# Layer 0 of a two-layer kernel: two DRAM places for the query and key halves, doubled key rows, and a new place for the weight loads and for GpSimd's low halves

## What is computed

```python
def _L0_xattn_ref(X, encoder_output, causal_mask, padding_mask, Wq, bq, Wk, bk, Wv, bv, Wo, bo):
    q = X @ Wq.T + bq                     # 32 heads of 8, in 8 groups of 4
    k = encoder_output @ Wk.T + bk        # 8 groups of 8
    v = encoder_output @ Wv.T + bv
    ...
    scores = jnp.einsum('bgrqd,bgkd->bgrqk', q, k) / jnp.sqrt(jnp.float32(HD))
    scores = jnp.where(causal_mask[None, None, None, :, :], -jnp.inf, scores)
    scores = jnp.where(padding_mask[:, None, None, None, :], -jnp.inf, scores)
    w = jax.nn.softmax(scores, axis=-1)
    out = jnp.einsum('bgrqk,bgkd->bgrqd', w, v)
    ...
    return out @ Wo.T + bo

def hbitlinear(x, w, bits):               # layer 0's feed-forward part: up, relu squared, down
    xq = act_quant(fwht(x), bits)         # Hadamard transform, then 8-bit rounding by the row's maximum
    wq = weight_quant(w)
    return jnp.einsum('bsd,fd->bsf', xq, wq)

x = x + jnp.tanh(g_xattn[0]) * _L0_xattn_ref(_layernorm(x, axis=-1), ctx_2048, ...)
x = x + jnp.tanh(g_ffn[0]) * _L0_ffn_ref(_layernorm(x, axis=-1), L0_ffn_w_up, L0_ffn_w_down)
```

## Time and profile before

| | us |
|---|---|
| median of 3 runs | 1274.64 (1269.18 to 1277.73) |
| the profiled execution | 1274.92 |
| its span, first to last instruction | 1272.9 |
| busy: PE, DVE, ACT, POOL | 1126.0, 1059.2, 918.8, 736.3 |
| mean granted TensorE clock | 0.967 |

### The profile page before, as it was taken

How to read it: one execution, slowest core, us unless ns; L and a number is a source line. 1 busy time by engine, 2 the same in 40 slices (tenths; PEclk the granted TensorE clock), 3 DMA queues, 4 the chain that set the end, 5 groups by cost and what they waited for, 6 DMA issues and landing times. The chain is left out here.

```text
span 1272.9 us, 30350 instructions
## 1 busy us (share of the span) xinstructions
PE 1126.0 (88%) x8831; PEld 909.1 (71%) x8831; DVE 1059.2 (83%) x2469; ACT 918.8 (72%) x3601; POOL 736.3 (58%) x1084
## 2 busy tenths in 40 slices
PE   2688888877899999999999999999899999659992
PEld 2345555544588888888888888888787788549981
DVE  6689999988798898998898888899689888766664
ACT  3556666658899889989989989987788888213330
POOL 5357777776756665665665665665445787323331
PEclk9889999999999999999999999999899999879996
DMA  6445554442230312220330220220311100633326
GB/s 165 88 81 78 84 77 79 76 69 49 72 105 1 88 32 57 87 66 21 87 87 0 87 87 0 87 87 31 110 52 59 35 35 31 254 95 82 96 68 202
DMA packets 135320, 97.04 MB, mean 76 GB/s; under 512 B 59070, under 2 KB 128832, under 8 KB 135233
## 3 DMA queue, kind: packets, MB, share of 16 engines
q1 hardware_dynamic: 125680, 84.18, 26.6%
q0 software_dynamic: 3408, 8.45, 1.8%
q10 hardware_dynamic: 6144, 3.35, 0.9%
HBM read 55.02 MB, written 41.56 MB: 76 GB/s over the span
## 5 line engine op out<-in xcount | busy, mean ns | idle before, releaser
L1543 POOL TENSOR_TENSOR head_rstd<-head_rstd,minus_half 128x4 f32<-128x4 f32 x192 | 224.8, 1171 | 15.0
L1531 ACT ACTIVATE squares<-ps 128x128 bf16<-128x128 f32 x768 | 202.5, 285 | 42.7 <-PE ps L1494 35.5
L1494 PE MATMUL ps<-w_proj_in,xq 128*128 128x512 f16 (+1 forms) x1024 | 209.9, 328 | 6.0 <-ACT headsT L1567 5.4
L1623 POOL TENSOR_TENSOR prob<-prob,rinv 128x512 f32<-128x512 f32 x128 | 140.5, 1098 | 109.0 <-DVE rinv L1618 108.8
L1610 ACT ACTIVATE prob<-ps,nmax 128x128 f32<-128x128 f32 x512 | 182.6, 391 | 9.6 <-DVE nmax L1601 8.2
L1567 ACT ACTIVATE headsT<-ps,l_hln 128x256 f32<-128x256 f32 (+1 forms) x256 | 168.2, 691 | 29.2 <-PE ps L1558 29.2
L1531 ACT ACTIVATION_READ_ACCUMULATOR squares<-ps 128x1 f32 x768 | 165.5, 216 | 0.0
L1551 DVE TENSOR_TENSOR heads_n<-ps,head_rstd 128x512 f32<-128x512 f32 x192 | 131.3, 684 | 25.0 <-POOL head_rstd L1543 24.8
L1494 PEld LDWEIGHTS ps<-w_proj_in,xq 128*128 (+1 forms) x1024 | 100.0, 98 | 53.3 <-issue 9.1
L1594 PE MATMUL ps<-headsT 128*128 128x128 f32 x1024 | 137.0, 277 | 1.1 <-DVE probT L1639 0.4
L1594 PEld LDWEIGHTS ps<-headsT 128*128 128x128 f32 x1024 | 128.9, 193 | 8.1 <-issue 5.5
(11 more groups left out here) (320 smaller groups left out, 2597.1 us busy)
## 6 DMA issues: line engine op xcount, KB each, us to landing
slots<-blank_slot SPq DMA_DIRECT2D x12, 1554.0 KB, 8.5
halves<-half_made SPq DMA_DIRECT2D x32, 256.0 KB, 2.5
w_proj_in<-halves SPq DMA_DIRECT2D x16, 512.0 KB, 9.0
w_out_raw<-in_wprojT SPq DMA_DIRECT2D x8, 512.0 KB, 3.9
half_raw<-in_winT SPq DMA_DIRECT2D x16, 256.0 KB, 3.0
half_raw<-in_woutT SPq DMA_DIRECT2D x16, 256.0 KB, 3.1
taken<-slots SPq DMA_DIRECT2D x15, 259.0 KB, 3.4
q_rows<-q_parts SPq DMA_DIRECT2D x48, 64.0 KB
```

What stands on the lines that cost most here:

```text
L1494: last = e.matmul(out, xq[:, k, which, slot_at], weights(k, hl, c0, n), start=(k == 0 and hl == 0), stop=(k == KD - 1 and hl == 1))
L1531: last = e.activation(squares[:, 4 * n + h, :], A[n][:, h * HD1:(h + 1) * HD1], ACT.Square, scale=HD1**-0.5, accum_out=hss[:, 4 * n + h:4 ...
L1543: e.tensor_tensor(hr[:, four], hr[:, four], t["half"][:, four], ALU.pow).then_inc(g_r[n].sem, 1)
L1623: e.tensor_tensor(prob[:, kind, :, :], prob[:, kind, :, :], spread(rinv[:, kind, :], P), ALU.mult).then_inc(g_p[kind].sem, 1)
```

## The change

`q_parts` and `k_parts` get a second place, by the parity of the element, and each key row is stored twice in a row (`k_parts` [2, 2, 64, 2, 128]). OUT writes the keys once for each copy (4 DMAs) and no longer waits for the reads of element i-1; INS and INT each wait for their own previous DMAs instead. `kT`'s layout goes from [half, group, token] to [group, half, token], so that INT reads both copies of a key row in one piece of 512 bytes: 6 DMAs in place of 9. On SP, LW moves from ahead of OUT to behind OUT and CT. On POOL, WL moves from ahead of F3b to behind it. In SP's start LW(0) keeps its early place.

```diff
-    "gpsimd": "XB+ F5v-- F1g- WL+ F3b- VC++ PD+ P1g++++ WC++ F7s-- F4v-",
-    "sync": "INS- ROW-- INT- LW OUT CT++",
+    "gpsimd": "XB+ F5v-- F1g- F3b- WL+ VC++ PD+ P1g++++ WC++ F7s-- F4v-",
+    "sync": "INS- ROW-- INT- OUT CT++ LW",
...
-    kT = sb("k_rows", [P, 2, 2, G0, P], F16)
+    kT = sb("k_rows", [P, 2, G0, 2, P], F16)
...
-    q_parts = nc.dram_tensor("q_parts", [2, D, P], F16, kind="Internal").ap()
-    k_parts = nc.dram_tensor("k_parts", [2, G0 * HD0, P], F16, kind="Internal").ap()
+    q_parts = nc.dram_tensor("q_parts", [2, 2, D, P], F16, kind="Internal").ap()
+    k_parts = nc.dram_tensor("k_parts", [2, 2, G0 * HD0, 2, P], F16, kind="Internal").ap()
...
     @s.piece("OUT", "sync")
     def _(e, i, p):
         e.wait_ge(v_part.sem, v_part.at(i))
-        e.wait_ge(d_ins.sem, d_ins.at(i - 1))
-        e.wait_ge(d_int.sem, d_int.at(i - 1))
         for part in range(2):
-            e.dma_start(q_parts[part].rearrange("(m p) t -> p m t", p=P), q_part[:, part, :, :]).then_inc(d_out.sem, 16)
-        e.dma_start(k_parts.rearrange("n f t -> f n t"), k_part[:, :, :]).then_inc(d_out.sem, 16)
+            e.dma_start(q_parts[p, part].rearrange("(m p) t -> p m t", p=P), q_part[:, part, :, :]).then_inc(d_out.sem, 16)
+        for hf in range(2):
+            e.dma_start(k_parts[p, :, :, hf, :].rearrange("n f t -> f n t"), k_part[:, :, :]).then_inc(d_out.sem, 16)
...
-    def of_group(k):
-        return k_parts[k].rearrange("(g d) t -> d g t", d=HD0)
+    def of_group(p, k):
+        return k_parts[p, k].rearrange("(g d) h t -> d g (h t)", d=HD0)
...
+        e.wait_ge(d_ins.sem, d_ins.at(i - 1))
         for hf in range(2):
-            e.dma_start(qm[0:GP, p, hf, :, :], q_parts[HI].rearrange("(g f) t -> f g t", f=GP)).then_inc(d_ins.sem, 16)
+            e.dma_start(qm[0:GP, p, hf, :, :], q_parts[p, HI].rearrange("(g f) t -> f g t", f=GP)).then_inc(d_ins.sem, 16)
...
+        e.wait_ge(d_int.sem, d_int.at(i - 1))
         for n, (q, k) in enumerate(parts):
-            for hf in range(2):
-                e.dma_start(kT[n * HD0:(n + 1) * HD0, p, hf, :, :], of_group(k)).then_inc(d_int.sem, 16)
-            e.dma_start(qT[n * HD0:(n + 1) * HD0, p, :, :], q_parts[q].rearrange("(h d) t -> d h t", d=HD0)).then_inc(d_int.sem, 16)
+            e.dma_start(kT[n * HD0:(n + 1) * HD0, p, :, :, :].rearrange("d g h t -> d g (h t)"), of_group(p, k)).then_inc(d_int.sem, 16)
+            e.dma_start(qT[n * HD0:(n + 1) * HD0, p, :, :], q_parts[p, q].rearrange("(h d) t -> d h t", d=HD0)).then_inc(d_int.sem, 16)
```

More of the change, by code:

```diff
@@ L437, in _ @@
         for hf in range(2):
-            last = e.activation(kT[LOW:P, 0, hf, :, :], tiled(low8[LOW:P, hf, :], G0), ACT.Copy, scale=UP)
+            last = e.activation(kT[LOW:P, 0, :, hf, :], tiled(low8[LOW:P, hf, :], G0), ACT.Copy, scale=UP)
         last.then_inc(laid, 1)
@@ L487, in _ @@
         for hf in range(2):
-            last = e.tensor_scalar(kT[LOW:P, 1, hf, :, :], tiled(low8[LOW:P, hf, :], G0), UP, 0.0, ALU.mult, ALU.add)
+            last = e.tensor_scalar(kT[LOW:P, 1, :, hf, :], tiled(low8[LOW:P, hf, :], G0), UP, 0.0, ALU.mult, ALU.add)
         last.then_inc(blocks, 1)
@@ L542, in _ @@
         e.memset(wk[:, :, G0 * HD0:P], 0.0)
-        e.memset(kT[0:TOP, :, :, :, :].rearrange("p s h g t -> p (s h g t)").bitcast(F32), 0.0)
+        e.memset(kT[0:TOP, :, :, :, :].rearrange("p s g h t -> p (s g h t)").bitcast(F32), 0.0)
         e.wait_ge(w_first, W_FIRST)
@@ L547, in _ @@
         e.tensor_scalar(bq[:, :], bq[:, :], HD0**-0.5, None, ALU.mult).then_inc(ready, 1)
-        e.memset(kT[TOP:LOW, :, :, :, :].rearrange("p s h g t -> p (s h g t)").bitcast(F32), UP_PAIR).then_inc(ready, 1)
+        e.memset(kT[TOP:LOW, :, :, :, :].rearrange("p s g h t -> p (s g h t)").bitcast(F32), UP_PAIR).then_inc(ready, 1)
         e.wait_ge(w_mask, W_MASK)
@@ L668, in layer0 @@
     d_ctx = sig("d_ctx", "sync", 16)
-    d_out, d_ins, d_int, d_row = sig("d_out", "sync", 16 * 3), sig("d_ins", "sync", 16 * 7), sig("d_int", "sync", 16 * 9), sig("d_row", "sync", 16 * 2)
+    d_out, d_ins, d_int, d_row = sig("d_out", "sync", 16 * 4), sig("d_ins", "sync", 16 * 7), sig("d_int", "sync", 16 * 6), sig("d_row", "sync", 16 * 2)
     pe_S, v_max = sig("pe_S", "tensor", G0), sig("v_max", "vector", G0)
@@ L812, in _ @@
         e.wait_ge(pe_S.sem, pe_S.at(i - 2))
+        e.wait_ge(d_ins.sem, d_ins.at(i - 1))
         for hf in range(2):
-            e.dma_start(qm[0:GP, p, hf, :, :], q_parts[HI].rearrange("(g f) t -> f g t", f=GP)).then_inc(d_ins.sem, 16)
+            e.dma_start(qm[0:GP, p, hf, :, :], q_parts[p, HI].rearrange("(g f) t -> f g t", f=GP)).then_inc(d_ins.sem, 16)
         for r in range(R0):
-            e.dma_start(kb[r * HD0:(r + 1) * HD0, p, :, r, :], of_group(HI)).then_inc(d_ins.sem, 16)
+            e.dma_start(kb[r * HD0:(r + 1) * HD0, p, :, r, :], of_group(p, HI)[:, :, 0:P]).then_inc(d_ins.sem, 16)
         e.dma_start(kb[TOP:TOP + 1, p, :, :, :].rearrange("o g r t -> o (g r) t"),
@@ L887, in _ @@
             some = slice(hf * HF, (hf + 1) * HF)
-            last = e.matmul(bank[:, :, some], kT[:, p, hf, g, :], qT[:, p, g * R0:(g + 1) * R0, some], start=True, stop=True)
+            last = e.matmul(bank[:, :, some], kT[:, p, g, hf, :], qT[:, p, g * R0:(g + 1) * R0, some], start=True, stop=True)
         last.then_inc(pe_ST.sem, 1)
```

## The result

| | before | changed |
|---|---|---|
| median, us | 1273.12 (1269.18 to 1277.73, 4 runs) | 1289.67 (1287.42 to 1292.45, 4 runs) |
| ratio to before | 1 | 1.013 (95% interval 1.0113 to 1.0147) |
| span of the profiled execution, us | 1272.9 | 1286.7 |
| round, mean of the ten between the marks of elements 5 and 15, us | 16.79 | 17.82 |
| mark of element 5 / of element 15, us | 105.07 / 272.96 | 112.30 / 290.46 |

The changed kernel is 1.3% slower. As before, a mark is the end of the last `k_part` row of `P3v`. The changed kernel's L786 is the same statement as before, and so are L983, L1021, L1151 and L1173; OUT is now L797 to L801.

The account below looks back on a forecast made before the run. DVE was taken to set the pace in layer 0, at 16.79 us a round. Ten rounds +17.8, start +4.3 and end 0 gave +22 us on 1274.92: 1297 us, range 1277 to 1312 (own range 1291 to 1309).

Parts of the forecast that it names:

- Two places and doubled rows: 0: SP's queue: OUT's wait for old reads (14.3 us in 8 rounds) goes, but DVE waits for none of it; worth 0.
- WL behind F3b: `yn` -1.80, `q` +1.72: DVE, each round: yn falls from 2.21 to 0.41 us, but WL then holds q of F6q (L1021), +1.72 us.
- rival 1: DVE against POOL: L1021 (q) gets ahead of WL and isn't held; 1278 us, chance 0.25.
- L = +8.3: Steady round: the unit load, behind OUT and CT, lands 8.3 us after the mark (bounds 8.05 and 9.55), delaying WM.
- I take 2.6: SP's unit load: assumed 2.6 us from issue to landing, near the fastest of 2.4 to 6.0, median 3.9.
- 10.30 from WM to the mark: DVE in a steady round: time from WM's start to the mark, 195.85 to 206.15, used in the round's sum.
- forecast round of 18.57: Steady layer 0 round: L + 0.05 + 10.30 - 1.80 + 1.72 = 18.57 us against 16.79, bounds 18.3 and 19.8.
- The start, +4.3: First elements: INS(3) lands some 3 us later; +2.5 us to element 4, +1.8 for the next round.
- its loop: Steady round: P3v(i), OUT(i), LW(i), WM(i), P3v(i+1), each waiting for the one before; sets the round.
- The end, 0: After the rounds: WM(15) waits for nothing new, one more yn may shrink; 0 to -2 us, taken as 0.
- Rival 2: Unit load lands in time, WM waits for nothing, yn gives back 1.80 us in some eleven rounds; 1255 us, chance 0.10.
- The checks it named: Layer 0: yn 0.41, L1021 some 2.1 us, idle 1 to 2.5 before L1151, SP's read wait gone, rounds some 18.6.

Follow-up runs that it names:

- e5: Kernel before with only the two DRAM places and doubled key rows (LW ahead of OUT, WL ahead of F3b): 1274.38 us, ratio 1.0000.
- e7: Kernel before (one place) with only LW moved behind OUT and CT: 1301.45 us, ratio 1.0212.
- e2: Changed kernel with WL back ahead of F3b on POOL: 1281.99 us, ratio 1.0077 to the kernel before.
- e1: Changed kernel with LW back ahead of OUT on SP: 1272.57 us, ratio 1.0002 to the kernel before.
- e6: Kernel before (one place, LW ahead of OUT) with only WL moved behind F3b: 1277.54 us, ratio 1.0024.
- e3: Changed kernel with WL on POOL also waiting for the end of the q it blocks: 1272.46 us, ratio 0.9993 to the kernel before.
- e8: Changed kernel with the unit loads of elements 1 to 3 ahead of OUT in the start alone: 1278.11 us, ratio 1.0043 to the kernel before.
- e4: Changed kernel with LW back ahead of OUT and WL waiting for the end of q: 1257.61 us, ratio 0.9879 to the kernel before.
- e9: Kernel before (one place, LW ahead of OUT) with WL behind F3b and behind q: 1263.61 us, ratio 0.9908.

## Why the prediction was right, and where its sizes were off

The forecast was 1297 us, slower, with 1277 to 1312; measured were 1290. The side and the mechanism held. The narrower range that it gave the forecast itself, 1291 to 1309, was missed by 1.3 us. Against the sum of 22.1 us (17.8 + 4.3), the rounds brought 7.5 less, the start 2.9 more and what follows the last mark 3.7 less: 13.8, the difference of the spans. So the total is nearer than its terms: 2.9 too little in the start made up for part of 11.2 too much in the rounds and the end.

- **Two places and doubled rows: 0.** Right as it stands (e5: 1.0000). The prediction counted the second place by OUT's missing wait behind the mark, and didn't say what it protects from: with the late load, WL ahead of F3b and one place the round is 18.26 (e7), with two 16.84 (e2). One place with both moves was not run. That wait is 19.0 us over the ten rounds, 4.7 more than in the earlier trace rows: two rounds have it ahead of L799 (SPq L799 <- DMA q_rows<-q_parts: 4.7, 2, 2.5). Nothing hangs on it.
- **WL behind F3b: `yn` -1.80, `q` +1.72.** Right. Measured -1.81 (2.199 to 0.393 in the medians) and +1.68 in the row shown. Over the ten rounds it is -1.70 and +1.70, because `yn` had been held for less than 2.2 us in four of the ten; the forecast took one round's figure. WL starts 1.82 us behind the end of `yn` where 1.86 was forecast, and `q` 0.30 us behind WL where 0.25 was. It holds in 11 rounds in a row, from 105.9 to 284.4 us. e1 and e6 show it without the late load, so rival 1 (`q` gets ahead of WL) is out, and e3 prices it at 1.60 us a round. It was closer than the 0.30 says: with the load in time WL leads by only 0.04 or 0.05 us in seven of ten rounds (e1), and one round of the changed kernel has 0.05. The Trainium skill, SBUF — State Buffer, section "Who interferes with whom", has the rule that of a VectorE instruction in a two-port mode and a GpSimd instruction the one that issues first keeps the shared pair of SBUF ports for its whole length. These rows agree: 0.30 us of lead, and even 0.05, hold `q` for the whole of WL.
- **L = +8.3: mis-sized.** OUT started at +0.03 as forecast and the last issue at +5.67 (forecast 5.65). What failed is the step "I take 2.6" for the landing: 2.1 is the median now, 1.8 the shortest, both below the bound that I had set by the earlier trace rows. I had said that the long landings ran beside INT's small reads, and still held the short end of the same rows for the least possible, though those rows too came from that place. WM started 7.79 us behind the mark on the mean over ten rounds, in place of 8.35.
- **10.30 from WM to the mark: one round's figure.** Over ten rounds of the kernel before it is 10.08 (16.79 less a mean of 6.71 from mark to WM). The changed kernel has 10.02: -0.06 where the terms say -0.08. So the forecast round of 18.57 was too long by 0.56 for L and 0.20 for this; 18.57 - 0.76 = 17.81, measured 17.82. Ten rounds: +10.3 us, not +17.8.
- **The start, +4.3: too small.** Measured +7.2 at element 5, and about 10 between the changed kernel and e8. The step that failed counted what lies between OUT(3) and INS(3) only. Each of WM(1) to WM(4) waits for its load, 12.8 us in all, and the prediction applied its loop only from element 4 on. It counted the one-time loads before CT(5) between OUT(3) and INS(3), but not that LW(3) now stands behind them too, as the changed kernel's SP queue shows (OUT(3) 74.30):

```profile
76.60 0.59 SPq L460 DMA_DIRECT2D l_lnw<-in_ln_w  x1
...
79.14 0.43 SPq L465 DMA_DIRECT2D l_smooth<-in_smooth  x1
...
82.51 0.43 SPq L1146 DMA_DIRECT2D unit_raw<-in_wvxT  x1
```

LW(3)'s last issue starts 8.2 us behind OUT(3) here, where a steady round has 5.6; WM(3) waits 3.84 us for it.

- **The end, 0.** At the mark of element 15 the changed kernel is 17.5 us behind, at the last row update of layer 0 17.0 and at the end of the span 13.8. Layer 1, which the change doesn't touch, took 914.8 us here and 918.0 before; over the eleven profiles it took 913.9 to 918.2. So the last 3 us are of the size of what one profile differs from another, and I don't assign them. The medians differ by 16.6.
- **Rival 2 (the load in time, 1255).** The load wasn't in time. Its price was near for a kernel that has both the load in time and no collision: e4 at 1257.6. The rival left the collision with `q` out: with the load in time alone (e1) the time is that of before.
- **The checks it named.** `yn` at 0.41 or less in all rounds, `q` of 2.1 us just behind WL, SP's wait gone: all seen. The idle time before L1151 is smaller, 1.1 us on the mean of nine waits (10.2/9), its longest 2.0. PE's share fell, and the clock stayed at 1.00, so that part of the doubt was idle. INS stayed hidden: no wait of PE for `k_blocks` is among the waits from 95 to 300 us.
- **Costs that don't add.** Nothing in the prediction depended on it, but my expectations of e2 and e7 did. From the rounds: late load alone with two places +0.05 (e2), WL's move alone +0.33 (e6), both +1.03.

## What to carry to other kernels

A long instruction that blocks another engine has to stand where that engine has nothing of the kind for its whole length. Moved by one piece it found the next victim; moved behind that one it gave 0.9% (e9), and 1.2% with two places (e4). Before a load is moved behind a write, count from the event that releases the write through every issue to the landing, in the steady rounds and in each of the first ones. Price parts in pairs: a stall may hide under a wait (e2), and a hidden wait may be laid bare by an edit elsewhere (e7).

## What the runs showed of the hardware

The time from issue to landing of the same six unit loads went with their place in the queue. Behind INT's reads, the medians of six kernels are 3.5 to 4.3 us, whether INT issues nine DMAs (before, e6, e9) or six with 512-byte pieces (e1, e4, e5); in e1:

```profile
DMA to landing us min/median/max: 2.6/4.1/5.6
```

Behind OUT and CT it is 2.1 in the changed kernel, in e2, e3 and e7. Which property of those reads slows them was not tried. And the length of a held DVE row isn't simply the blocker's. `q` took 2.11 us when WL had started 0.30 us ahead, 2.18 when 0.23 ahead, and 2.35 to 2.37 when 0.04 or 0.05 ahead (one round of the changed kernel, seven of the ten of e1): it ends 0.28 or 0.29 us behind WL each time. `yn` of the earlier trace rows ended 0.15 behind (199.16 against 199.01).
